# Block 0 of a gated cross-attention kernel put in another order, and a causal table in rounded form

## The reference

```python
def xattn(query, ctx, Wq, Wk, Wv, Wo):                 # query: B x 2048 x 512, ctx: B x 77 x 512, B = 2
    q, k, v = heads(query @ Wq.T), heads(ctx @ Wk.T), heads(ctx @ Wv.T)      # 16 heads of 32
    scores = einsum('bhqd,bhkd->bhqk', q, k) * 32 ** -0.5
    scores = where(arange(2048)[:, None] >= arange(77)[None, :], scores, -1e9)
    return einsum('bhqk,bhkd->bhqd', softmax(scores), v) @ Wo.T

x = x + tanh(g_xattn) * xattn(layernorm(x), ctx, Wq, Wk, Wv, Wo)
h = layernorm(x)
x = x + tanh(g_ffn) * ((silu(h @ Wg.T) * (h @ Wu.T)) @ Wd.T)                 # 1536 hidden, int weights / 127
```

## Time and profile before

| | |
|---|---|
| median of 3 runs | 898.4 us (898.28 to 899.2) |
| the profiled execution | 898.39 us, span 896.6 us |
| mean granted clock of TensorE | 0.992 |
| busy: PE, DVE, ACT, POOL | 865.3, 654.6, 460.9, 398.6 us |
| end of block 0 on TensorE (first unit of block 1) | 81.33 us |

### The profile page before, as it was taken

One profiled execution on the slowest core, in us unless ns is written; L12 is line 12 of the kernel. 1 busy time (PEld: TensorE's weight loads), 2 busy tenths in 40 slices (PEclk: granted clock), 3 DMA queues, 4 the chain that ended last, 5 costly groups with the idle time before them and its releaser, 6 DMA issues.

```text
span 896.6 us, 12906 instructions
## 1 busy us (share of the span) xinstructions
PE 865.3 (97%) x4121; PEld 715.2 (80%) x4121; DVE 654.6 (73%) x1082; ACT 460.9 (51%) x1130; POOL 398.6 (44%) x340
## 2 busy tenths in 40 slices
PE   8878999999999999999999999999999999999997
PEld 6656878888888878778888888888888888888876
DVE  3757778686868687759878758687578787487782
ACT  3656656675766755636426536146264165362450
POOL 3234556564656465347414615235434156242250
PEclk9998999999999999999999999999999999999999
DMA  9202393636364631438613336324256043244212
GB/s 323 67 14 95 118 320 114 222 104 213 125 192 157 218 123 53 158 119 310 241 41 124 129 112 237 133 87 159 94 186 248 16 149 130 89 144 156 82 42 96
DMA packets 60407, 128.75 MB, mean 144 GB/s; under 512 B 7616, under 2 KB 20416, under 8 KB 60352
## 3 DMA queue, kind: packets, MB, share of 16 engines
q1 hardware_dynamic: 59488, 127.00, 41.1%
q10 hardware_dynamic: 864, 1.05, 0.4%
HBM read 99.93 MB, written 27.79 MB: 142 GB/s over the span
## 4 chain that ended last, share of the span: by engine, by line
PE 84%; DVE 8%; ACT 5%; issue 2%; POOL 1%; DVEq 0%; POOLq 0%; ACTq 0%
PE psum L1766 33%; PE psum L1506 27%; PE psum L1816 18%; PE psum L1531 3%; ACT e L770 3%; DVE e L1044 1%; DVE mx L1041 1%; DVE bn L1002 1%; PE psum L1631 1%; DVE pT L1015 1%; PE psum L1620 1%; PE psum L1615 1%; POOL hT L675 1%; DVE mx L1052 1%; DVE K L1093 1%
## 5 line engine op out<-in xcount | busy, mean ns | idle before, releaser
L1766 PE MATMUL psum<-xv,ring 128*128 128x512 f32 x1344 | 308.2, 390 | 0.9 <-ACT a L932 0.7
L1766 PEld LDWEIGHTS psum<-xv,ring 128*128 128x128 f32 x1344 | 251.3, 188 | 55.3 <-ACT a L932 1.1
L1816 PE MATMUL psum<-w_d,hT 128*128 128x512 f32 x768 | 177.7, 390 | 1.2 <-POOL hT L675 0.7
L675 POOL TENSOR_TENSOR hT<-th,hT 128x512 fp32r<-128x512 f32 x48 | 86.6, 1805 | 200.9 <-ACT hT L952 200.9
L1816 PEld LDWEIGHTS psum<-w_d,hT 128*128 128x128 f32 x768 | 143.6, 188 | 32.7 <-POOL hT L675 2.0
L549 POOL TENSOR_TENSOR e<-e,rden 128x616 f32<-128x616 f32 x64 | 77.9, 1217 | 128.9 <-DVE rden L1075 77.2
L770 ACT ACTIVATE e<-psum,nmx,q_scale 128x77 f32<-128x77 f32 x256 | 102.6, 427 | 9.6 <-DVE nmx L1056 9.6
L920 ACT ACTIVATE a<-psum 128x512 f32<-128x512 f32 x48 | 28.7, 599 | 131.7 <-PE psum L1766 131.4
L1506 PE MATMUL psum<-wo,aT 128*128 128x512 f32 x384 | 95.1, 398 | 0.5 <-DVE aT L1026 0.5
L1386 DVE SCALAR_TENSOR_TENSOR acc<-psum,gate_ffn,acc 128x512 f32<-128x512 f32 x64 | 47.6, 749 | 65.1 <-PE psum L1816 65.1
L1506 PE MATMUL psum<-xT,wq 128*128 128x512 f32 x360 | 92.2, 408 | 1.2 <-DVE qT L1026 1.2
(11 more groups left out here) (107 smaller groups left out, 1196.6 us busy)
## 6 DMA issues: line engine op xcount, KB each, us to landing
ring<-w_var SPq DMA_DIRECT2D x48, 896.0 KB, 4.7
w_var<-stage SPq DMA_DIRECT2D x12, 896.0 KB, 4.6
x_ln<-x SPq DMA_DIRECT2D x32, 256.0 KB, 5.0
x_res<-x SPq DMA_DIRECT2D x32, 256.0 KB, 5.1
x_mid<-x_res SPq DMA_DIRECT2D x32, 256.0 KB, 2.0
x<-x_mid SPq DMA_DIRECT2D x16, 512.0 KB, 5.7
acc<-x_mid SPq DMA_DIRECT2D x16, 512.0 KB, 6.3
out<-acc SPq DMA_DIRECT2D x32, 256.0 KB, 2.0
```

The lines of the kernel that those rows point to most:

```text
L675: nc.gpsimd.tensor_tensor(hT[:, 1, i % HH, j, :], h[:, :], hT[:, 0, i % HH, j, :].bitcast(f32), ALU.subtract).then_inc(h_lo, 1)
L1766: last = nc.tensor.matmul(psum[:, bank, :], stat, mov, start=start and j == 0, stop=j == len(terms) - 1, skip_group_check=not start)
L1816: last = nc.tensor.matmul(m_bank[t % 2][:, :], hT[:, a, m, t // TT, (t % TT) * P:(t % TT + 1) * P], w_d[:, HH * h + m, :], start=m == 0 an ...
```

## The change

- **Loads.** Wq's quarters are issued first, on both queues. Wk goes from SyncE's queue to ScalarE's, behind Wq and ahead of x's quarters 2 and 3. x's quarters 0 and 1 stand behind the context on SyncE's. Wo is loaded ahead of block 1's x.
- **TensorE.** 8 warm-up products, Wq's mean, 12 more idle products (`BRIDGE`), the four keys, then Q for m = 2 and 3 (`FIRST` = 2, 3, 0, 1), the values of the first sequence, unit 1 of tile 0, Q for m = 0 and 1, and so on, unit 1 ahead of unit 0 in every tile. The values go to the transposes' banks, with semaphores of their own (`vk_full`, `vk_free`), and TensorE waits for both copies (`vk_free` = 2) ahead of the first transpose.
- **VectorE and ScalarE.** Centring first, x's split after it; two statistics ahead of the keys' remainders; shift1 and denominator1 ahead of shift0 and denominator0 in tiles 0 to 2; all maxima ahead of the remainders that can wait. Both halves of Wo are split ahead of the first exponent. The statistics of block 1 stand together.
- **GpSimd.** The remainders of V for b = 0 (`v_low_rows(0)`) move from VectorE to GpSimd, between the third and the fourth tile's weighing. The upper unit is weighed first.
- **The mask.** The identity and the causal table are copied to f32r once, and the mask's product uses the copies (in blocks 0 and 4).
- The wait for the scale is made for every tile, not for t = 0 alone.

```diff
-    WARM = 24
+    WARM, BRIDGE = 8, 12
+    FIRST = (2, 3, 0, 1)
@@ sync: loads
             for k in range(KD // 2):
-                sp.dma_start(xs[:, k, :], xt_f[0, :, k, :]).then_inc(xs_in[k], 16)
-            for k in range(KD // 2):
                 sp.dma_start(wq_stage[:, k, :], wq_t[k * P:(k + 1) * P, :]).then_inc(wq_in[k], 16)
             sp.dma_start(ctx_stage[:, :, :], ctx_t.rearrange("(k p) n -> p k n", p=P)).then_inc(ctx_in, 16)
-            sp.dma_start(wk_stage[:, :, :], wk_t.rearrange("(k p) n -> p k n", p=P)).then_inc(wk_in, 16)
+            for k in range(KD // 2):
+                sp.dma_start(xs[:, k, :], xt_f[0, :, k, :]).then_inc(xs_in[k], 16)
             load_x(0, first=True)
             sp.dma_start(wv_stage[:, :, :], wv_t.rearrange("(k p) n -> p k n", p=P)).then_inc(wv_in, 16)
+            sp.dma_start(x_res[:, :, :], wo_t.rearrange("(k p) n -> p k n", p=P)).then_inc(wo_in, 16)
             load_xs(1)
-            sp.dma_start(x_res[:, :, :], wo_t.rearrange("(k p) n -> p k n", p=P)).then_inc(wo_in, 16)
@@ gpsimd
+            nc.gpsimd.tensor_copy(ident_r[:, :], ident[:, :]).then_inc(consts_ready, 1)
+            pool.wait_ge(mask_built, 1)
+            nc.gpsimd.tensor_copy(causal_r[:, :, :], causal[:, :, :]).then_inc(consts_ready, 1)
...
+            weigh(0, 0, 1)
             x_low_t(1, (0, 1))
-            probabilities(0, 0)
+            weigh(0, 1, 1)
+            weigh(0, 0, 0)
             x_low_t(1, (2, 3))
-            probabilities(0, 1)
-            probabilities(0, 2)
-            probabilities(0, 3)
+            weigh(0, 1, 0)
+            weigh(0, 2, 1)
+            weigh(0, 2, 0)
+            v_low_rows(0)
+            weigh(0, 3, 1)
+            weigh(0, 3, 0)
@@ scalar
             for k in range(KD // 2, KD):
+                act.dma_start(wq_stage[:, k, :], wq_t[k * P:(k + 1) * P, :]).then_inc(wq_in[k], 16)
+            act.dma_start(wk_stage[:, :, :], wk_t.rearrange("(k p) n -> p k n", p=P)).then_inc(wk_in, 16)
+            for k in range(KD // 2, KD):
                 act.dma_start(xs[:, k, :], xt_f[0, :, k, :]).then_inc(xs_in[k], 16)
...
+            wq_high(0)
+            wq_high(1)
+            wq_high(2)
+            x_high_t(0, 0)
+            wq_high(3)
+            x_high_t(0, 1)
+            x_high_t(0, 2)
+            x_high_t(0, 3)
...
+            for m in FIRST:
+                k_high(m)
             query0(0)
             query0(1)
+            wo_high(0)
+            wo_high(1)
+            # first_block, new order:
+            #   exp1(0,0) with query0(2) between, query0(3), x_high_t(1,0..1), exp1(0,1), exp0(0,0), x_high_t(1,2..3),
+            #   p(0,0), exp0(0,1), p(0,1), p(0,2), exp1(0,2), exp0(0,2), p(1,0..2), q(0), v_high(0),
+            #   exp1(0,3), exp0(0,3), q(1), p(2,0), p(2,1), q(2), p(2,2), p(3,0), q(3), p(3,1), p(3,2), v_high(1)
@@ vector
+            # centre and wq_low, then x_low_t(0..3), stats(0,0..1), k_low(2), k_low(3), stats(0,2..3),
+            #   query0(0), query0(1), k_low(0), k_low(1); first_block, new order:
+            #   v_copy(0), shift1(0,0), denominator1(0,0), query0(2), query0(3), shift1(0,1), shift0(0,0),
+            #   denominator1(0,1), denominator0(0,0), v_copy(1), shift0(0,1), p(0,0), denominator0(0,1), p(0,1), p(0,2),
+            #   slot_free(0,2), shift1(0,2), shift0(0,2), denominator1(0,2), denominator0(0,2), p(1,0), p(1,1),
+            #   slot_free(0,3), shift0(0,3), p(1,2), shift1(0,3), q(0), stats(1,0..3), denominator1(0,3),
+            #   denominator0(0,3), q(1), p(2,0), p(2,1), q(2), p(2,2), p(3,0), q(3), p(3,1), p(3,2)
@@ tensor
-                        terms.append((ident[:, :], causal[:, :, :].rearrange("p h k -> p (h k)")))
+                        terms.append((ident_r[:, :], causal_r[:, :, :].rearrange("p h k -> p (h k)")))
...
+            idle_products(WARM)
             pe.wait_ge(avg_ready, 1)
...
+            idle_products(BRIDGE)
+            pe.wait_ge(ctx_in, 16)
+            pe.wait_ge(wk_in, 16)
+            for m in FIRST:
+                keys(m)
...
                 pe.wait_ge(wv_in, 16)
                 batch_values(0)
+                unit(0, 1, 2)
+                query(2, FIRST[2])
+                query(3, FIRST[3])
+                unit(1, 1)
+                unit(0, 0, 4)
+                batch_values(1)
+                unit(1, 0)
+                unit(2, 1)
+                pe.wait_ge(vk_free, B)
                 p(0, 0)
                 p(0, 1)
+                unit(2, 0)
                 p(0, 2)
                 pe.wait_ge(x_lo, 8)
                 q(0)
+                p(1, 0)
+                p(1, 1)
+                unit(3, 0)
+                p(1, 2)
                 unit(3, 1)
                 q(1)
+                p(2, 0)
                 p(2, 1)
+                q(2)
                 p(2, 2)
                 p(3, 0)
+                q(3)
                 p(3, 1)
                 p(3, 2)
```

More of the change, by code:

```diff
@@ L115, in flamingo_gated_block @@
         causal = sb("causal", [P, HG, SK])
+        ident_r = sb("ident_r", [P, P], f32r)
+        causal_r = sb("causal_r", [P, HG, SK], f32r)
         gates = sb("gates", [P, 2])
@@ L1113, in centre, with query0 @@
                     .then_inc(wq_centred, 1)
-            def query0(m):
-                q_low(m + 1, m)
-            for k in range(KD):
-                x_low_t(k)
+            def query0(i):
+                m_low(i + 1, i, qT[:, 1, FIRST[i], :], qT[:, 0, FIRST[i], :])
             dve.wait_ge(wq_mean, 1)
@@ L1128, in _ @@
             wq_low(3)
+            for k in range(KD):
+                x_low_t(k)
+            stats(0, 0)
+            stats(0, 1)
+            k_low(2)
+            k_low(3)
+            stats(0, 2)
+            stats(0, 3)
             query0(0)
@@ L1132, in _ @@
             k_low(1)
-            for t in range(TT):
-                stats(0, t)
-            query0(2)
             def first_block():
@@ L1141, in v_copy @@
                 def v_copy(b):
-                    dve.wait_ge(m_full, V_AT + b + 1)
-                    nc.vector.tensor_copy(v_keys[0:SK, b], m_bank[b % 2][0:SK, :]).then_inc(m_free, 1)
+                    dve.wait_ge(vk_full, b + 1)
+                    nc.vector.tensor_copy(v_keys[0:SK, b], t_bank[b][0:SK, :]).then_inc(vk_free, 1)
                 def q(m):
                     q_low(5 + m, m)
-                shift0(0, 0)
-                k_low(2)
-                k_low(3)
-                query0(3)
-                denominator0(0, 0)
-                shift0(0, 1)
+                v_copy(0)
                 shift1(0, 0)
                 denominator1(0, 0)
-                v_copy(0)
+                query0(2)
+                query0(3)
+                shift1(0, 1)
+                shift0(0, 0)
+                denominator1(0, 1)
+                denominator0(0, 0)
+                v_copy(1)
+                shift0(0, 1)
+                p(0, 0)
                 denominator0(0, 1)
-                p(0, 0)
-                shift1(0, 1)
                 p(0, 1)
-                denominator1(0, 1)
                 p(0, 2)
                 slot_free(0, 2)
+                shift1(0, 2)
                 shift0(0, 2)
+                denominator1(0, 2)
+                denominator0(0, 2)
                 p(1, 0)
-                denominator0(0, 2)
-                v_copy(1)
-                shift1(0, 2)
                 p(1, 1)
-                denominator1(0, 2)
-                p(1, 2)
                 slot_free(0, 3)
                 shift0(0, 3)
+                p(1, 2)
+                shift1(0, 3)
+                q(0)
+                for t in range(TT):
+                    stats(1, t)
+                denominator1(0, 3)
                 denominator0(0, 3)
-                q(0)
+                q(1)
                 p(2, 0)
-                shift1(0, 3)
-                q(1)
                 p(2, 1)
-                stats(1, 0)
-                stats(1, 1)
-                denominator1(0, 3)
+                q(2)
                 p(2, 2)
-                q(2)
-                v_low_rows(0)
                 p(3, 0)
+                q(3)
                 p(3, 1)
-                stats(1, 2)
-                stats(1, 3)
-                q(3)
                 p(3, 2)
@@ L1617, in turn, with idle_products @@
                 last.then_inc(xb_full, 1)
-            for _ in range(WARM):
-                nc.tensor.matmul(t_bank[0][:, 0:P], ident[:, :], ident[:, :], start=True, stop=True)
+            def idle_products(count):
+                for _ in range(count):
+                    nc.tensor.matmul(t_bank[0][:, 0:P], ident[:, :], ident[:, :], start=True, stop=True)
+            idle_products(WARM)
             pe.wait_ge(avg_ready, 1)
@@ L1625, in _ @@
             last.then_inc(wq_mean, 1)
+            idle_products(BRIDGE)
[3 more added lines that the diff above has]
+                keys(m)
             for k in range(KD):
+                pe.wait_ge(w_split, k + 1)
```

(15 more changed lines are left out.)

110 lines of the change are left out of this document (42 added, 68 removed).

## The result

The changed kernel takes 887.31 us (median of 4 runs, 887.13 to 887.69) against 898.5 us before (898.28 to 899.2): ratio 0.9874, 95% interval 0.9862 to 0.9886, 11.2 us less. The forecast was 885.4 us, in a range of 881 to 890; 883 to 888 us had the chance of 0.55. The profiled execution has a span of 885.5 us against 896.6 us, 11.1 us less.

A forecast was written before the change was run, and what follows sets the result against it. It took TensorE's stream and its waits, loose in block 0, as the bound. 11.6 us saved before block 1 plus 1.4 us in block 4 make 13.0 us: 898.4 to 885.4 us, range 881 to 890 us.

The forecast's parts named there:

- What bounds: Whole kernel: TensorE's stream and waits bound it; a microsecond saved before block 1's first score unit is one off the end.
- Front: Start of block 0: Wq's mean ends 3.9 us sooner; first exponent row at 28.2 us instead of 39.77, 11.6 us gained.
- rival 2: Late front: Wk or x lands late, or Q's pair runs at half clock; 887.5 to 890.5 us, chance 0.20.
- Bridge: Idle TensorE passes after Wq's mean: 24 at 0.148 us, 3.55 us to 11.95 us, when TensorE has nothing else.
- Values ahead of the first score cost 1.25 us: Block 0, TensorE: the first values, 3.45 us to 25.2 us, put off the first score by 1.25 us.
- Tiles: Block 0's four exponent rows start at 28.2, 34.9, 45.5 and 57.1 us, 28.9 us from first to last.
- I am wrong ... if the spacing of the four exponent rows grows beyond 29 us in all: Block 0: a sign that the prediction fails, spacing of the four exponent rows beyond 29 us in all.
- Rival 3: Block 0: VectorE blocked behind each exponent row, 3.3 us a tile, 13.2 us lost; 898.6 to 900 us, chance 0.04.
- Collision: Block 0, fourth tile: GpSimd's V remainders lock out VectorE's negated maximum; exponent at 57.1 us, not 54.4, 2.7 us lost.
- Clock in q(3): End of block 0: the last Q taken at half clock after TensorE idles, 4.35 us; full clock would save 1.5 us.
- Sum: Whole kernel: 11.6 us gained up to block 1 and 1.4 us in block 4, 13.0 us, giving 885.4 us.
- every offset is the old one: From block 1's start at 69.7 us on, all times keep their old distance, apart from block 4's 1.4 us.

The follow-up runs named there:

- 5: The changed kernel with the old load order (x, then Wq; Wk on SyncE's queue behind the context; Wo keeps its new place): 892.28 us, ratio 0.9915.
- 6: The kernel before with the new load order alone (Wq first, Wk behind it on ScalarE's queue, x later): 902.06 us, ratio 1.0041.
- 4: The changed kernel without the 12 idle products between Wq's mean and the keys: 887.34 us, ratio 0.986.
- 1: The changed kernel with V's upper part and remainders one tile earlier, behind the third negated maximum: 884.12 us, ratio 0.9826.
- 2: The changed kernel with V's first remainders back on VectorE, behind p(3,0): 884.09 us, ratio 0.983.
- 3: The changed kernel with the mask's products on the full float32 tables again, in blocks 0 and 4: 888.34 us, ratio 0.9884.
- 8: On top of 1, the fourth tile's unit with the eight exponents also goes first on TensorE and VectorE: 884.21 us, ratio 0.9823.
- 10: 1, 8 and 9 together, in the changed kernel: 883.45 us, ratio 0.9819.
- 11: On top of 9, block 1's four statistics moved behind the maxima of the first three exponent rows: 882.78 us, ratio 0.9819.
- 9: On top of 1, Wo's remainders moved into GpSimd's idle time of block 0, V's second upper part ahead of p(2,2): 882.60 us, ratio 0.9804.
- 12: 11 with the fourth tile's exponents first, as in 8: 880.12 us, ratio 0.9795.

## Why the prediction was right, and where it was off

- **What bounds**: right. Block 0 gained 10.4 us, the time from block 1 on changed by 0.7 us, and each microsecond at block 1 was one at the end, but for 0.8 us of the 10.4 (below).
- **Front**: right in size. 3.6 us at the centring (3.8 walked), 11.4 at the first exponent row (11.6). The load order is a needed part of it (5: 3.7 to 5.0 us lost without it) and worthless without the order of work (6: 3.3 us lost). The order of work alone gives 7.1 us (5 against the kernel before). Wk landed in time (in 4 TensorE waits for it to 11.52 us, in the changed kernel the keys start at 11.20 us without a wait) and the granted clock was 1.00 up to 22 us, so rival 2 fell.
- **Bridge**: right that it lies beside the path; it was in fact not needed for the clock either (4). Its passes took 0.12 us, not 0.148, since the 7.10 us of the earlier trace rows contain a slow start: now the first 16 passes took 3.5 us and the 24 of the bridge 2.8. So warm-up ended at 5.1 us instead of 4.1, which put the mean 0.2 us later than walked, and the keys started 0.8 us sooner than walked, which gained nothing: from centring to the first negated maximum it is 19.4 us, with and without the bridge.
- **Values ahead of the first score cost 1.25 us**: wrong, and without effect. They ended at 24.1 us, with Q's remainders (24.02 us), and VectorE came to the score only at 27.2 us.
- **Tiles**: this is the step that was mis-sized, and by the prediction's own sign ("I am wrong ... if the spacing of the four exponent rows grows beyond 29 us in all") it failed: from the first to the fourth row it is 30.1 us, where the walk had 28.9. The walk was right to 0.1 us at the second row, ran 1.0 us short at the third and 1.4 at the fourth. At the third it is the way through the first transposes: GpSimd's weighing ended at 41.34 us and not at 40.95, and from there to the third exponent row it took 5.1 us and not 4.55, with VectorE idle for 0.58 us ahead of the first remainder of p, for ScalarE's upper part. The sign was set only 0.1 us above the walk's own spacing, and the miss is small against the range: 1.2 us at block 1. Rival 3 fell all the same: 2.8 of the 30.1 us are the collision, and without them the rows stand 27.3 us apart, closer than the 28.1 us of before.
- **Collision**: right in place, kind and price (the negated maximum 3.00 us long, walked as 2.85). 1 and 2 removed it in two ways, and each gave 3.2 us (4.3 and 4.0 by the ratios), which includes up to 1.6 us of q(3) at full clock; by places the collision alone is 2.8 us. But the margin was thin: GpSimd started at 54.91 us, 0.53 us ahead of the negated maximum. The lock that "SBUF — State Buffer" of the Trainium skill describes (section "SBUF: two separate sides") fits the rows read here. Both long negated maxima end with GpSimd's instruction (58.44 and 58.40 us, 76.92 and 76.89 us). VectorE's own V remainders in 2, with both inputs in SBUF, are lengthened under GpSimd's Wo, and the second Wo in turn under them.
- **Clock in q(3)**: taken as half, and it was (4.36 us in the chain). That was luck in part, for the order doesn't fix it: in kernels 3 and 4, which have the same order behind the front, it was full (3.01 and 3.02 us, behind waits of 1.50 and 2.79 us), and in 5 mostly half (4.07 us, behind 2.78 us).
- **Sum**: 13.0 us walked, 11.2 measured. The term that was too large is block 0's, 11.6 for 10.4: the 1.4 us of the fourth row less 0.1 behind it. Block 4's mask gave 1.30 us directly (3.63 to 2.33), and the value products behind it 0.25 (8.42 to 8.17), for 1.4; that the value products get shorter was in no term, and why they do isn't shown. The rest is "every offset is the old one", which was not quite so: the lead of 10.4 us at the start of block 1 is 9.8 at its third Q (119.79 to 110.02) and 9.6 in block 4. The largest piece of the 0.8 us is at that Q, where TensorE waits 1.08 us instead of 0.71 for VectorE:

```profile
110.02 3.02 PE L1520 MATMUL psum<-xT,wq 128*128 128x512 f32 x12 [1.08 <-DVE qT L1047]
```

and VectorE's aggregate of block 3's first statistic stood 0.51 us behind its own predecessor, where such gaps are 0.15 us:

```profile
107.11 0.68 DVE L1023 BATCH_NORM_STATS2 bn<-x_ln 128x6 f32<-128x512 f32 x1
108.30 0.18 DVE L1026 BATCH_NORM_AGGREGATE mv<-bn 128x2 f32<-128x6 f32 x1 [0.51 <-DVE bn L1023]
...
109.21 0.18 DVE L1026 BATCH_NORM_AGGREGATE mv<-bn 128x2 f32<-128x6 f32 x1 [0.15 <-DVE bn L1023]
```

What held that one instruction wasn't tried. The other 0.4 us went in pieces of 0.2 us and less.

## What to carry to other kernels

Walk a hand-made order engine by engine with measured durations, but add what each hand-over to another engine costs by the trace (here 1.0 us was missing by the third tile), and look at what GpSimd does at the moment of every small VectorE instruction on the path. A saving that shows nothing may stand beside a second link of the same length: look for the engine that has no gap after it, and try both together. Where a stretch runs now at full and now at half clock, compare places ahead of it and not totals alone. Compare places inside a stage from a mark behind the loads, because the front alone moved by 1.5 us between profiles.

## What the runs showed of the hardware that I had not expected

- The first 16 idle passes of 128 columns took 3.5 us (0.22 each), though the windows from 0 us on list a granted clock of 1.00; 24 later ones took 2.8 us (0.12 each).
- The clock of q(3) isn't fixed by the wait ahead of it. It ran at half clock (4.58 and 4.59 us) behind waits of 2.77 us in the changed kernel and in 8, and mostly at half behind 2.78 us in 5 (4.07 us) and 1.59 us in 10 (4.24 us); at full clock (3.00 to 3.02 us) behind 2.79 us in 4, 2.18 us in 11 and 1.50 us in 3. Behind 0.7 us (2, 9, 12) and behind none (1) it was full each time.
- The 36 value products of block 1 took 9.2 us in kernels with a wait of 0.4 us for VectorE among them (the changed kernel and 1), and 8.2 us in those without it (9 to 12), all at a granted clock of 1.00. The difference is more than twice the wait; the rest of it has no cause shown.
